# A graph-attention and expert kernel: the sums' wait for zeroed PSUM banks, on every second tile and one zeroing later

## The chip, the cores and the metric

The kernel runs on one core of a Trainium2 chip. The metric is the device time of one launch in microseconds (us), the median of several runs. TensorE (PE in the profile, PEld for its weight loads) multiplies matrices, VectorE (DVE), ScalarE (ACT) and GpSimd (POOL) work elementwise or gather, SyncE (SP) issues transfers. Each engine works through its own list of instructions in order, and waits on semaphores for the others.

## The reference

A graph layer over 6250 nodes and 100,000 edges sorted by destination, then an expert layer with eight experts of which each node uses two. What matters here is the graph layer's last step, a sum of messages over the edges of each destination node:

```
h = jnp.einsum('ni,hid->nhd', x, W)
...
alpha = jnp.exp(e_stable)
alpha_sum = jax.ops.segment_sum(alpha, dst, num_segments=N)
alpha_norm = alpha / (alpha_sum[dst] + 1e-08)
msg = alpha_norm[:, :, None] * h_src
out_h = jax.ops.segment_sum(msg, dst, num_segments=N)
...
for e in range(E):
    h = jax.nn.gelu(tokens @ w1[e] + b1[e], approximate=False)
    y = h @ w2[e] + b2[e]
    out = out + combine[:, e:e + 1] * y
```

## The kernel before

A first part (to about 144 us) normalizes x, multiplies it with the weights into a table of 260 columns per node in HBM, and cuts the edges into tiles of 128 that belong to blocks of 125 nodes. The second part works in 52 rounds of 16 tiles, 832 tiles in all. The loops of all engines run over a round `it` and a step `k` (the tile of that round), and the order in which the code lists the work of a step is the order on that engine; nothing else sets it.

In a round, GpSimd gathers the table rows of the edges for a round three ahead (L753, `ring`). VectorE and TensorE work out the softmax arguments of the next round in a chain that goes back and forth: TensorE's D (L1121, sixteen small matmuls at step 0), VectorE's `eC` (L803 to L807), TensorE's transpose (L1129, step 3), VectorE's scans, TensorE's L1132 (step 5), L1138 and L1139 (step 7), L1142 (step 9), VectorE's `arg`, ScalarE's exponentials (L1416 to L1418, step 10), VectorE's messages (L863, steps 11 to 14). At step k TensorE adds tile k into a PSUM bank: L1164, a matmul of the tile's one-hot matrix `oh` with its messages, 128 x 260, in float32, which the chip runs in two passes. It is called sum k below. Three banks `agg_ps` are taken in turn, by the block that a tile belongs to; the bank's number is loaded from a table.

ScalarE's `evacuate` at step k waits until sum k - 1 is done (semaphore `agg`), copies the bank of the tile before to `acc` (L1396), and zeroes the bank into which a coming block will be added (L1398, "zeroing k" below), which counts up `zr`. Each step has one copy and one zeroing, whether or not a block ends there. In front of sum 0 TensorE also waits for VectorE's rescaling of a bank (`rs`, L856), in front of sum 12 for a one-hot matrix. `zr` counts all zeroings of the kernel, so `zr` at least t means that the zeroing of step t - 1, over all rounds, is done.

From round 4 on the expert layer runs in the same steps, three rounds for each group of three blocks, 17 groups. TensorE's `hidden` (L1191, six matmuls) and `output` (L1237, four matmuls) stand between the sums, and ScalarE's GELU (L1427) between the zeroings; `prepare` (L1243, L1273, L1294, L1296) readies the next group's blocks. VectorE adds the outputs up (L998). Rounds 7, 8 and 9 are the first three with the experts' matmuls of a group in them, and the pattern repeats every three rounds until round 51. Rounds 28, 29 and 30 are such a set: it runs from 922.55 to 1003.16 us.

Of the kernel before, what the change touches and what calls it, by code (L numbers as in the profile page):

```python
# [22 lines left out]
def gnn_ffn_kernel(nc, x, src, dst, W, attn, W_out, rw, w1, b1, w2, b2, out):  # L23
# [46 lines left out]
    with ExitStack() as ctx:  # L70
# [26 lines left out]
        with ExitStack() as st:  # L97
# [3 lines left out]
            def sem(name):  # L101
                return st.enter_context(nc.semaphore("p_" + name))
# [469 lines left out]
        with ExitStack() as st:  # L572
# [3 lines left out]
            def sem(name):  # L576
# [71 lines left out]
            S = {n: sem(n) for n in (  # L648
                "lk init am zr otc D e eT x1m X CC CBp rho rT arg wm sc al oh msg rs agg ev "
                "w1c w1l on tt oc pj x1 va sq xk tu uh ul rt lgc dif exr cm ct cc cs b2 yb yd yi h1 gl y2 ya st tops").split()}  # L650
# [34 lines left out]
            with nc.Block() as block:  # L685
# [414 lines left out]
                def _(pe):  # L1100
# [50 lines left out]
                    def aggregate(b, k):  # L1151
                        t, q = b * BT + k, k // 4
                        if k == 0:
                            if b > 0:
                                pe.wait_ge(S["rs"], b)
                            else:
                                pe.wait_ge(S["oh"], QUADS - 1)
                        elif k == 12:
                            pe.wait_ge(S["oh"], QUADS * b + QUADS + (1 if b + 1 < NBAT else 0))
                        if t == 0:  # L1160
                            pe.wait_ge(S["am"], 1)
                        elif t > 1:
                            pe.wait_ge(S["zr"], t - 1)
                        T.matmul(bank_of[k // 8][k % 8], oh[:, (4 * b + q) % OHQ, k % 4, :], rings[b % RING][:, k, :],  # L1164
                                 start=False, stop=True, skip_group_check=True).then_inc(S["agg"], 1)

# [12 lines left out]
                    def edges(it, k):  # L1179
                        if it + 1 < NBAT:  # L1180
                            chain(it + 1, k)
                        if 0 <= it < NBAT:
                            aggregate(it, k)
# [346 lines left out]
```

## Time and profile before

| | us |
|---|---|
| runs (three), median | 1638.88 |
| runs, lowest and highest | 1637.24, 1646.97 |
| profiled execution | 1644.37 |
| its span, first to last instruction | 1642.6 |
| TensorE busy with matmuls | 1358.9 (83%) |
| VectorE busy | 1106.4 (67%) |
| ScalarE busy | 990.5 (60%) |
| GpSimd busy | 837.5 (51%) |

The span is 1.8 us shorter than the profiled execution's own time, which in turn is 5.5 us over the median of the runs. Matmuls are pipelined and their ends in the profile are modelled, so that rows of TensorE that follow each other overlap a little.

### The profile page before, as it was taken

To read this page: it belongs to the slowest core of one execution; us is meant where nothing else is said; L and a number is where in the kernel's file an instruction comes from. 1 tells how busy PE (TensorE), PEld (TensorE's weight loads), DVE (VectorE), ACT (ScalarE), POOL (GpSimd) and SP (SyncE) were. 2 spreads that over 40 slices of the span, in tenths; PEclk is the share of its full clock that TensorE was granted. 3 is DMA by queue.
4 is the path that set the end of the run, shared out by engine and by line. 5 is a ranking of instruction groups with operands and counts; after the bars stand their busy time and mean duration, and the time that the engine had idled before them with its cause. 6 is when DMAs were issued, how large, how long until landed. Compare 5 with 4: busy or idle time off the path is not lost.

```text
span 1642.6 us, 25322 instructions
## 1 busy us (share of the span) xinstructions
PE 1358.9 (83%) x7177; PEld 1114.8 (68%) x7177; DVE 1106.4 (67%) x3062; ACT 990.5 (60%) x2522; POOL 837.5 (51%) x886
## 2 busy tenths in 40 slices
PE   5741575578989888998999889899988888998998
PEld 3630343467777777777777777777777777777887
DVE  6522464667777777777676768687867677777643
ACT  3530444457666666766676767676767576767733
POOL 1237465656565555655555555555555555552000
PEclk9775566889999999999999999999999999999999
DMA  9355354333434343434343434343433333456000
GB/s 218 95 153 143 102 154 117 102 107 96 126 97 122 97 124 104 117 104 115 104 115 103 115 106 115 104 113 106 114 106 111 104 107 106 115 101 80 1 17 16
DMA packets 89793, 174.56 MB, mean 106 GB/s; under 512 B 22471, under 2 KB 56081, under 8 KB 89625
## 3 DMA queue, kind: packets, MB, share of 16 engines
q0 software_dynamic: 40448, 111.89, 26.8%
q1 hardware_dynamic: 48103, 60.78, 12.5%
q8 instruction: 60, 0.98, 0.2%
q14 instruction: 76, 0.62, 0.1%
q10 hardware_dynamic: 1106, 0.27, 0.1%
HBM read 159.26 MB, written 14.43 MB: 106 GB/s over the span
## 4 chain that ended last, share of the span: by engine, by line
PE 45%; ACT 14%; DVE 14%; another core or an unknown queue 11%; issue 8%; ACTq 2%; DVEq 0%
PE agg_ps L1164 14%; PE ob L1237 13%; PE hb L1191 10%; ACT acc L1396 4%; ACT agg_ps L1398 3%; PE ob L1273 2%; ACT hT L1427 2%; DVE ring L863 2%; DVE oh L798 2%; DVE y L998 1%; ACT L1427 1%; ACT L1409 1%; PE ob L1302 1%; ACTq L662 1%
## 5 line engine op out<-in xcount | busy, mean ns | idle before, releaser
L753 POOL DMA_INDIRECT ring<-table,srcE x832 | 805.4, 968 | 596.0 <-PE agg_ps L1164 294.7
L1164 PE MATMUL agg_ps<-ring,oh 128*128 128x260 f32 x1664 | 539.6, 423 | 32.4 <-ACT agg_ps L1398 15.0
L1396 ACT COPY acc<-agg_ps x831 | 307.6, 370 | 322.1 <-issue 123.1
L1237 PE MATMUL ob<-w_sb,hT 128*125 128x256 f32 x1600 | 413.6, 384 | 32.7 <-DVE y L998 16.2
L1164 PEld LDWEIGHTS agg_ps<-ring,oh 128*128 128x128 f32 x1664 | 305.6, 205 | 87.4 <-issue 27.3
L1237 PEld LDWEIGHTS ob<-w_sb,hT 128*125 128x125 f32 x1600 | 294.4, 188 | 96.5 <-issue 26.6
L1398 ACT COPY agg_ps<-zc 128x260 f32 x832 | 314.6, 378 | 28.6 <-issue 2.3
L863 DVE TENSOR_TENSOR ring<-ring,kbank 128x1024 f32<-128x1024 f32 x208 | 244.7, 1214 | 46.3 <-ACT ring L1417 44.8
L998 DVE SCALAR_TENSOR_TENSOR y<-ob,cmb,y 125x256 f32<-125x256 f32 x400 | 189.1, 476 | 100.0 <-remote 47.0
L1427 ACT ACTIVATE hT<-hb,b_sb 128x375 f32<-128x375 f32 (+1 forms) x272 | 154.0, 566 | 120.1 <-PE hb L1191 95.6
L1191 PE MATMUL hb<-xTh,w1l 128*128 128x376 f32 (+1 forms) x544 | 188.9, 429 | 0.0
L798 DVE TENSOR_TENSOR oh<-kbank,relE 128x512 f32<-128x512 f32 x208 | 141.0, 678 | 4.4 <-PE agg_ps L1164 2.4
L1191 PE MATMUL hb<-xTl,w1h 128*128 128x376 f32 (+1 forms) x544 | 138.5, 336 | 0.0
L1191 PE MATMUL hb<-xTh,w1h 128*128 128x376 f32 (+1 forms) x544 | 137.5, 335 | 0.0
L1191 PEld LDWEIGHTS hb<-xTh,w1l 128*128 128x128 f32 x544 | 103.7, 194 | 15.6
L803 DVE TENSOR_REDUCE dsum<-kbank 128x64 f32<-128x192 f32 x52 | 18.6, 358 | 139.4 <-remote 133.5
L1191 PEld LDWEIGHTS hb<-xTh,w1h 128*128 128x128 f32 x544 | 99.3, 192 | 0.0
L1191 PEld LDWEIGHTS hb<-xTl,w1h 128*128 128x128 f32 x544 | 99.0, 192 | 0.0
L1129 PE MATMUL kbank<-ident,eC 128*64 128x128 f32 x52 | 16.0, 308 | 89.9 <-DVE eC L807 63.4
L761 POOL TENSOR_TENSOR rstd<-mv,root_ 125x3 f32<-125x3 f32 (+1 forms) x17 | 14.8, 871 | 124.3 <-DVE mv L927 123.5
L1129 PEld LDWEIGHTS kbank<-ident,eC 128*64 128x64 f32 x52 | 5.9, 113 | 103.2 <-DVE eC L807 73.5
L486 PE MATMUL bank<-wcat,xnT 128*125 128x264 f32 x200 | 60.2, 429 | 14.5 <-issue 6.4
(285 smaller groups left out, 1461.8 us busy)
## 6 DMA issues: line engine op xcount, KB each, us to landing
OT<-relb_d SPq DMA_DIRECT2D x52, 512.0 KB
ring<-table,srcE POOLq DMA_INDIRECT x832
y<-in_x_dram SPq DMA_DIRECT2D x50, 125.0 KB
out_dram<-y SPq DMA_DIRECT2D x50, 125.0 KB
table<-hrow SPq DMA_DIRECT2D x25, 227.5 KB
acc<-in_x_dram SPq DMA_DIRECT2D x2, 1568.0 KB
acc<-in_L_ffn_w_dram SPq DMA_DIRECT2D x1, 2048.0 KB
w_sb<-in_L_ffn_w_dram SPq DMA_DIRECT2D x1, 2048.0 KB
```

The source lines that it names most:

```text
L486: m = T.matmul(bank[2 + b % 3][0:Q, 0:WIDE], xnT[:, b % 2, k, :], wcat[:, k, :], start=k == 0, stop=k == KC - 1)
L753: pool.indirect_dma_start(out=rings[b % RING][:, k, :], out_offset=None, in_=table[:, :], in_offset=bass.IndirectOffsetOnAxis(ap=srcE[:, t ...
L798: v.tensor_tensor(oh[:, (4 * b + q) % OHQ], iota_ps.unsqueeze(1).to_broadcast([P, 4, P]), relE[:, t0:t0 + 4].unsqueeze(2).to_broadcast([P, ...
L863: v.tensor_tensor(m, m, al.to_broadcast([P, 4, H, DH]), ALU.mult).then_inc(S["msg"], 1)
L998: v.scalar_tensor_tensor(y[0:Q, u, i, :], o[0:Q, 0:D], cmb[0:Q, u, i, e:e + 1], y[0:Q, u, i, :], ALU.mult, ALU.add).then_inc(S["ya"], 1)
L1164: T.matmul(bank_of[k // 8][k % 8], oh[:, (4 * b + q) % OHQ, k % 4, :], rings[b % RING][:, k, :], start=False, stop=True, skip_group_check= ...
L1191: t = T.matmul(out_, a, b_, start=j == 0, stop=j == len(terms) - 1)
L1237: t = T.matmul(o[0:Q, 0:D], hT[:, e % 2, f, cols], w2_sb[:, e, f, :], start=f == 0, stop=f == KC - 1)
L1273: t = T.matmul(ob1[0:Q, j * D:(j + 1) * D], oT[:, j, k, :], wout_sb[:, k, :], start=k == 0, stop=k == KC - 1)
L1396: A.copy(row_of[h][k % 8], closed[h][k % 8]).then_inc(S["ev"], 1)
L1398: A.copy(coming[h][k % 8], zc[:, 0:1].to_broadcast([P, ROW])).then_inc(S["zr"], 1)
L1427: A.activation(hT[:, e % 2, f, 0:w], hbank[f][:, 0:w], ACT.Gelu, bias=b1_sb[:, e, f:f + 1]).then_inc(S["gl"], 1)
```

## The change

One condition in `aggregate` is changed. Let t be the number of a tile over all rounds. Before, every sum from t = 2 on waits for `zr` at least t - 1. Now the sums of even t wait for `zr` at least t, and those of odd t have no wait on `zr`. A round has 16 tiles, so even t is even k.

```diff
                         if t == 0:
                             pe.wait_ge(S["am"], 1)
-                        elif t > 1:
-                            pe.wait_ge(S["zr"], t - 1)
+                        elif t > 1 and t % 2 == 0:
+                            pe.wait_ge(S["zr"], t)
                         T.matmul(bank_of[k // 8][k % 8], oh[:, (4 * b + q) % OHQ, k % 4, :], rings[b % RING][:, k, :],
                                  start=False, stop=True, skip_group_check=True).then_inc(S["agg"], 1)
```

415 sums (t = 2, 4, ... 830) wait for one more zeroing than before, 415 (t = 3, 5, ... 831) lose their wait. A waiting sum holds its weight load, which is issued first. No instruction of any engine is added, removed or moved. On TensorE, at the start of a round of the kind of round 29 (its D, then sums 0 to 3 with what stands between them), before the change:

```order
L1121 MATMUL kbank<-d3,OT 128x12 x15
L1164 MATMUL agg_ps<-ring2,oh 128x260 [waits e_zr,e_rs]
L1164 MATMUL agg_ps<-ring2,oh 128x260 [waits e_zr]
L1243 MATMUL ob1<-ident,xn 128x125 [waits e_ya]
L1243 MATMUL ob1<-ident,xn 128x125
L1164 MATMUL agg_ps<-ring2,oh 128x260 [waits e_zr]
L1191 MATMUL hb0<-xTh,w1l 128x376 [waits e_gl]
...
L1129 MATMUL kbank<-ident,eC 64x128 [waits e_e]
L1164 MATMUL agg_ps<-ring2,oh 128x260 [waits e_zr]
L1237 MATMUL ob0<-w2_sb,hT 125x256 [waits e_ya,e_gl]
```

The same place now:

```order
L1121 MATMUL kbank<-d3,OT 128x12 x15
L1164 MATMUL agg_ps<-ring2,oh 128x260 [waits e_zr,e_rs]
L1164 MATMUL agg_ps<-ring2,oh 128x260
L1243 MATMUL ob1<-ident,xn 128x125 [waits e_ya]
L1243 MATMUL ob1<-ident,xn 128x125
L1164 MATMUL agg_ps<-ring2,oh 128x260 [waits e_zr]
L1191 MATMUL hb0<-xTh,w1l 128x376 [waits e_gl]
...
L1129 MATMUL kbank<-ident,eC 64x128 [waits e_e]
L1164 MATMUL agg_ps<-ring2,oh 128x260
L1237 MATMUL ob0<-w2_sb,hT 125x256 [waits e_ya,e_gl]
```

Nothing moved: sums 1 and 3 lost their wait. Sum 2's wait, the third L1164, reads the same but asks for zeroing 1 now, where it asked for zeroing 0.

## Rows read from the trace of the kernel before

**Rows 1.** Page, costliest groups: count | busy us, mean ns | idle us before them, releaser.

```profile
L1164 PE MATMUL agg_ps<-ring,oh 128*128 128x260 f32 x1664 | 539.6, 423 | 32.4 <-ACT agg_ps L1398 15.0
L1396 ACT COPY acc<-agg_ps x831 | 307.6, 370 | 322.1 <-issue 123.1
...
L1398 ACT COPY agg_ps<-zc 128x260 f32 x832 | 314.6, 378 | 28.6 <-issue 2.3
...
L1427 ACT ACTIVATE hT<-hb,b_sb 128x375 f32<-128x375 f32 (+1 forms) x272 | 154.0, 566 | 120.1 <-PE hb L1191 95.6
```

**Rows 2.** Windows, middle and early rounds: us, busy by engine, PEclk, DMA share, GB/s.

```profile
352.00:1540.00 1188.00, 1068.38 (x5847) 893.58 (x5848) 880.02 (x2416) 804.91 (x2008) 667.35 (x690) 0.99 0.40 107
144.00:352.00 208.00, 119.76 (x462) 80.45 (x462) 107.36 (x271) 90.86 (x259) 122.96 (x128) 0.66 0.41 114
```

**Rows 3.** Windows, rounds 28 to 30, the same columns.

```profile
922.55:1003.16 80.61, 72.26 (x402) 60.58 (x403) 60.37 (x167) 54.79 (x138) 47.17 (x50) 1.00 0.39 111
```

**Rows 4.** Timeline, round 28, tile 4: start us, us, what [idle before <-releaser].

```profile
928.64 0.60 PE L1164 MATMUL agg_ps<-ring,oh 128*128 128x260 f32 x2
...
929.10 0.38 ACT L1398 COPY agg_ps<-zc 128x260 f32 x1
...
931.53 0.71 PE L1164 MATMUL agg_ps<-ring,oh 128*128 128x260 f32 x2 [0.33 <-issue]
```

**Rows 5.** Timeline, round 28, tile 12.

```profile
940.61 0.30 PEld L1164 LDWEIGHTS agg_ps<-ring,oh 128*128 128x128 f32 x2 [0.28 <-issue]
...
941.22 0.38 ACT L1398 COPY agg_ps<-zc 128x260 f32 x1
```

**Rows 6.** Timeline, round 29, tile 2.

```profile
950.55 0.60 PE L1164 MATMUL agg_ps<-ring,oh 128*128 128x260 f32 x2
...
951.68 0.50 PE L1191 MATMUL hb<-xTh,w1h 128*128 128x376 f32 x2
...
951.96 0.38 ACT L1396 COPY acc<-agg_ps  x1 [2.37 <-PE agg_ps L1164]
...
952.37 0.38 ACT L1398 COPY agg_ps<-zc 128x260 f32 x1
...
952.89 0.30 PE L1129 MATMUL kbank<-ident,eC 128*64 128x128 f32 x1 [0.71 <-issue]
```

**Rows 7.** Timeline, round 29, tile 14.

```profile
969.92 0.61 PE L1164 MATMUL agg_ps<-ring,oh 128*128 128x260 f32 x2
...
970.28 0.38 ACT L1398 COPY agg_ps<-zc 128x260 f32 x1
...
972.99 0.45 PE L1237 MATMUL ob<-w_sb,hT 128*125 128x256 f32 x1 [1.00 <-issue]
```

**Rows 8.** Timeline, round 30, tile 2.

```profile
978.71 0.60 PE L1164 MATMUL agg_ps<-ring,oh 128*128 128x260 f32 x2
...
979.15 1.03 PE L1237 MATMUL ob<-w_sb,hT 128*125 128x256 f32 x4
...
980.38 0.38 ACT L1398 COPY agg_ps<-zc 128x260 f32 x1
...
980.90 0.30 PE L1129 MATMUL kbank<-ident,eC 128*64 128x128 f32 x1 [0.73 <-DVE eC L807]
```

**Rows 9.** Timeline, round 30, tile 14.

```profile
997.37 0.60 PE L1164 MATMUL agg_ps<-ring,oh 128*128 128x260 f32 x2
...
998.36 0.38 ACT L1398 COPY agg_ps<-zc 128x260 f32 x1
...
998.79 0.71 PE L1164 MATMUL agg_ps<-ring,oh 128*128 128x260 f32 x2
...
1002.05 0.41 PE L1121 MATMUL kbank<-d,OT 128*128 x10 [1.52 <-DVE oh L798]
```

**Rows 10.** Timeline, round 3 of the first seven, tile 2.

```profile
252.01 0.38 ACT L1398 COPY agg_ps<-zc 128x260 f32 x1
...
252.53 0.42 PE L1129 MATMUL kbank<-ident,eC 128*64 128x128 f32 x1 [6.50 <-DVE eC L807]
```

## The prediction

> **What bounds the kernel now.** I read the page's groups first, then the busy time by stage, then the timeline of three rounds in which the pattern repeats. In what follows sum k is TensorE's L1164 for tile k of a round, and zeroing k is ScalarE's L1398 in its step k of the same round. Before, sum k waits for zeroing k-2. In the changed kernel an even sum waits for zeroing k-1, and an odd sum waits for none. The page's row of the sums says that TensorE stood idle 32.4 us in all in front of them, of which 15.0 us ended with a zeroing [rows 1]: the present wait is nearly free. From 352 to 1540 us TensorE is busy 1068.38 of 1188.00 us, and its clock is at 0.99; ScalarE is busy 804.91 us [rows 2]. So the long middle is TensorE's, with 120 us of idle time in it, or 8.35 us in the three rounds from 922.55 to 1003.16 us [rows 3]. ScalarE is no bound by its share, but it runs behind TensorE, and today it may be a tile further behind than after the change. What the change costs is therefore the lateness of zeroing k-1 against sum k, for even k, less what TensorE idles shortly afterwards anyway.
>
> **The wait that is removed.** Odd sums lose a wait. Its price can't be over the 15.0 us of [rows 1] for odd and even together, since the next even sum asks for more than the odd one did. Below nothing is excluded, because nothing is added there. I take zero: where an odd sum waits today, the even one in front of it waits for the same zeroing after the change.
>
> **The wait that is moved forward**, place by place in rounds 28 to 30, which stand for 15 such groups of three (rounds 7 to 51). TensorE works in order, so behind a waiting sum its own hidden, output and step matmuls queue, and VectorE's chain and ScalarE's GELUs wait for those.
>
> Round 28, tile 4: zeroing 3 ends at 929.10 + 0.38 = 929.48, the sum started at 928.64 [rows 4]. With its weight load behind the wait it starts about 929.6, 0.95 late. TensorE's idle time before tile 6, 0.33 us, gives that much back: 0.6 stays.
>
> Tile 10 of round 28, and tile 6 of rounds 29 and 30, have a loop: hidden matmuls, GELU, copy, zeroing, next even sum. The ScalarE part is 566 + 370 + 378 ns = 1.31 us and some handovers [rows 1]; TensorE has a sum and an output between, 998.79 - 997.37 = 1.42 us from one sum to the next [rows 9]. Between nothing and 0.5 us each; I take 0.25, since the two are nearly equal.
>
> Round 28, tile 12: weight load 940.61, zeroing 11 ends 941.60 [rows 5], 1.0 late as it stands. But this zeroing is behind ScalarE's exponentials and a GELU that waited for TensorE's hidden matmuls, so ScalarE will come some 0.7 later by itself (the 0.6 and 0.25 above). TensorE is then 1.7 behind, which contains the earlier shifts and is the round's sum.
>
> Round 29, tile 2, the dearest: ScalarE waited 2.37 us for TensorE's sums before its copy at 951.96, and zeroing 1 ends at 952.75; sum 2 ran at 950.55 [rows 6]. It moves to about 952.83, 2.3 late. In front of L1129 TensorE has 0.71 us idle now. Sum 2 and the hidden matmuls take 952.18 - 950.55 = 1.63 us, so L1129 moves from 952.89 to about 954.45: 1.55 is left. L1129 feeds VectorE's softmax chain, so the chain moves with it. With the loop, 1.8.
>
> Round 29, tile 14: zeroing 13 ends at 970.66, the sum was at 969.92, 0.85 late with its load; 1.00 us of idle time follows before the output at 972.99 [rows 7] and takes it. Between 0 and 0.85, I take 0.
>
> Round 30, tile 2: the same as in round 29 with output matmuls in place of hidden ones. Zeroing 1 ends 980.76, sum 2 moves from 978.71 to 980.84, and with 1.47 us of work (979.15 + 1.03 - 978.71) L1129 comes at 982.2 instead of 980.90 [rows 8], 1.3 late. Tile 14: zeroing 13 ends 998.74 against 997.37, 1.4 late, and 1.52 us of idle time before L1121 at 1002.05 covers it, unless what that waits for moves along [rows 9]. Between 0 and 1.4, I take 0.4, nearer to the cover. With the loop 1.95.
>
> The group: 1.7 + 1.8 + 1.95 = 5.45 us, times 15 = 82 us. **The first seven rounds** are paced otherwise, with TensorE idle 6.50 us before L1129. Zeroing 1 ends at 252.39, L1129 starts at 252.53 [rows 10]. Sum 2 now stands between, 0.8 us at the slow clock, so L1129 is 0.7 later: 7 x 0.7 = 5 us. **Sum:** 1644.37 + 82 + 5 = 1731 us for the profiled execution. That execution is 5.5 us above the median of the runs, 1638.88, so in runs as shown 1726 us, 5.3% slower.
>
> **A page weighed against the rows.** The largest terms hang on when TensorE's sums are known to be done. By the modelled ends, sums 0 and 1 are over when sum 2 starts at 950.55, while ScalarE's copy, which needs only sum 0, got its signal 1.4 us later [rows 6]. The Trainium skill, Perfetto Trace Analysis, section Tensor Engine Instruction, states that the end reported for TensorE is estimated from the instruction's size and that the semaphore is pushed only after PSUM acknowledges. The trace agrees, and adds that it can be over a microsecond here. If the modelled ends were the truth, zeroing 1 would end near 951.4 and both tile 2 terms would vanish into the idle time, leaving 2.6 us a group, 39 us and a time of 1683. I go by the signal.
>
> **Rivals.** (a) *Given back.* The idle time at the end of rounds 29 and 30 (1.00 and 1.52 us, [rows 7, 9]) and before L1129 belongs to signals that do not move with TensorE. Then the shifts of the rounds are swallowed there too: 5.45 - 2.5 - 1.0 for the chain, about 2 us a group, 30 + 5 us, 1674. For it: VectorE and ScalarE have spare time. Against: what they wait for is mostly TensorE's own result. (b) *Nothing given back.* All six places at their full lateness, 1.0 + 1.0 + 2.3 + 0.85 + 2.1 + 1.4, and 1 us for the loops, 9.65 us a group: 145 + 5, 1789. For it: VectorE's chain shifts too, and ScalarE's lag is renewed by each GELU. Against: 8.35 us of idle time a group is there to be used. (c) *The clock.* In the rounds from 144 to 352 us TensorE is busy 119.76 of 208 us and its granted clock averages 0.66, a mix of the levels of 1.2 and 2.4 GHz, against 0.99 in the middle [rows 2]. The added waits lower its share in the middle from 0.90 to about 0.84. If that costs a twentieth of the clock, 1068 us of work grow by about 50, on top of the forecast: 1776. The Trainium skill, TensorE: Matmul & The Clock Gate, section What's actually happening, says that the array runs at 1.2 GHz after idling and at 2.4 GHz once busy; by it the longer stalls in rounds 29 and 30 would be the ones to fall. (d) *No effect.* Once TensorE has waited for a few zeroings it is no longer ahead, the later even waits find theirs done, and what was lost lies inside idle time: 1640. Against it stand three zeroings that end over 1 us after their sum began. (e) *Faster.* The odd sums' loads start at once, and the 15.0 us of waiting for zeroings goes without a new one: 1624. It decides from the point at which every even sum finds zeroing k-1 done; [rows 4 to 9] show six that do not, so it has little for it.
>
> **How the numbers follow.** Forecast 0.54 (1726, own range 1700 to 1760), given back 0.17, nothing given back 0.12, clock 0.08, no effect 0.06, faster 0.03. The range 1666 to 1790 holds the forecast, most of (a) and (b), and (c); what is left out is (d), (e) and the tails. A difference of 1%, 16 us, is about what a measurement of this kernel tells from none. Slower by more than that: the first four less the low tail of (a), 0.88; same 0.09; faster 0.03.
>
> **What would show it.** In the changed kernel's profile the idle time in front of L1164 that ended with a zeroing should go from 15.0 us to 150 us or more, and lie at tiles 2, 4, 12 and 14. TensorE's busy time should stay within 1%. L1129 should come right after hidden or output matmuls in rounds of the kinds of 29 and 30, with its idle time gone. A group of three rounds should take 86 us instead of 80.6. If it takes 83 or less, (a) is right; if the granted clock of the middle is under 0.97, (c) is in it. The forecast is wrong in kind if the signals of sums 0 and 1 come earlier once TensorE has less queued behind them, since that lateness was measured with it running ahead.

## The result and the profile after

The changed kernel takes 1722.07 us (median of 4 runs, 1713.95 to 1725.43) beside 1638.06 us for the kernel before (4 runs, 1633.63 to 1646.97): a ratio of 1.0487, with a 95% interval of 1.0458 to 1.0516. The forecast was 1726. The profiled execution took 1720.34 us, 76.0 more than that of the kernel before.

The page of the changed kernel, costliest groups, as in [rows 1]: count | busy us, mean ns | idle us before them, releaser.

```profile
L753 POOL DMA_INDIRECT ring<-table,srcE x832 | 805.5, 968 | 671.7 <-PE agg_ps L1164 409.6
L1164 PE MATMUL agg_ps<-ring,oh 128*128 128x260 f32 x1664 | 555.3, 430 | 200.9 <-ACT agg_ps L1398 152.6
L1396 ACT COPY acc<-agg_ps x831 | 307.1, 370 | 334.1 <-PE agg_ps L1164 118.3
```

The idle time in front of the sums went from 32.4 to 200.9 us, and what of it ended with a zeroing from 15.0 to 152.6. The copies and zeroings themselves are as long as before.

The changed kernel's waits of TensorE: waited for, us in total, times, longest us.

```profile
PE agg_ps L1164 <- ACT agg_ps L1398: 152.6, 89, 22.1
PE agg_ps L1164 <- issue: 47.8, 57, 2.1
PE kbank L1121 <- issue: 26.0, 7, 12.7
PE kbank L1129 <- issue: 17.9, 1, 17.9
```

The same view of the kernel before, for the two step matmuls that idled most:

```profile
PE kbank L1129 <- DVE eC L807: 63.4, 17, 19.3
PE kbank L1129 <- issue: 26.4, 11, 19.2
PE kbank L1121 <- DVE oh L798: 18.6, 14, 1.8
PE kbank L1121 <- issue: 17.7, 6, 11.9
```

So not all of the new waiting is new. L1129's idle time fell from 89.8 to 17.9 us: TensorE now waits before it gets there, in front of sum 2. One such wait alone is 22.1 us long and lies in the first seven rounds, which have become hardly longer: from the start of round 0 to the start of round 7 it was 203.2 us before and is 204.5 now (149.89 to 353.12, and 150.34 to 354.85). The 76 us came behind that. The last sum ends at 1643.19 us in place of 1567.20.

Windows of the changed kernel: the middle, the early rounds, rounds 28 to 30; columns as in [rows 2, 3].

```profile
352.00:1620.00 1268.00, 1103.95 (x5890) 909.16 (x5889) 887.51 (x2428) 811.16 (x2014) 668.24 (x691) 0.97 0.37 100
144.00:352.00 208.00, 112.41 (x439) 71.00 (x440) 107.60 (x271) 91.83 (x260) 122.99 (x128) 0.71 0.41 114
...
967.26:1053.81 86.55, 75.02 (x409) 61.71 (x405) 60.19 (x164) 54.11 (x135) 48.91 (x50) 0.98 0.37 104
```

The group of three rounds takes 86.55 us in place of 80.61. TensorE is busy 75.02 in it where it was 72.26, and idle 11.5 where it was 8.35. Over the whole program it is busy 1383.5 us where it was 1358.9, 1.8% more.

The same from the start of round 7 to the start of round 49, which is fourteen groups of three and the same work in both kernels; first before, then after:

```profile
353.12:1495.95 1142.83, 1026.33 (x5628) 859.03 (x5629) 846.75 (x2324) 772.09 (x1925) 665.04 (x688) 0.99 0.41 109
354.87:1566.82 1211.95, 1054.85 (x5634) 868.69 (x5632) 847.99 (x2320) 773.63 (x1923) 663.55 (x686) 0.97 0.38 103
```

These fourteen groups take 69.1 us more. TensorE's idle time makes 40.6 us of that (116.5 before, 157.1 after), and 28.5 us is longer busy time at a lower granted clock. So a group is 4.9 us longer, of which 2.9 are idle time and 2.0 busy time.

Timeline of the changed kernel, round 29, tile 2, beside [rows 6]: start us, us, what [idle before <-releaser].

```profile
998.73 0.36 DVE L803 TENSOR_REDUCE dsum<-kbank 128x64 f32<-128x192 f32 x1 [0.88 <-PE kbank L1121]
1000.18 0.38 ACT L1396 COPY acc<-agg_ps  x1 [2.39 <-PE agg_ps L1164]
1000.59 0.38 ACT L1398 COPY agg_ps<-zc 128x260 f32 x1
1001.02 0.30 PEld L1164 LDWEIGHTS agg_ps<-ring,oh 128*128 128x128 f32 x2 [2.35 <-ACT agg_ps L1398]
...
1002.26 0.51 PE L1191 MATMUL hb<-xTh,w1h 128*128 128x376 f32 x2
...
1002.61 0.27 PE L1129 MATMUL kbank<-ident,eC 128*64 128x128 f32 x1
```

It is the picture of [rows 6] with the sum on the other side of the wait. ScalarE's copy still comes 2.39 us after it was free, zeroing 1 ends at 1000.97, and 0.05 us later the load of sum 2 starts, 2.35 us late. L1129 now follows the hidden matmuls without idle time.

Round 29, tile 14, beside [rows 7]:

```profile
1019.91 0.38 ACT L1398 COPY agg_ps<-zc 128x260 f32 x1
1020.34 0.30 PEld L1164 LDWEIGHTS agg_ps<-ring,oh 128*128 128x128 f32 x2 [1.36 <-ACT agg_ps L1398]
...
1023.45 1.10 PE L1237 MATMUL ob<-w_sb,hT 128*125 128x256 f32 x4 [0.94 <-DVE y L998]
```

The sum's weight load waits 1.36 us for zeroing 13, and the idle time before the output matmuls, which was to take that up, is still there in this round: 0.94 us, beside 1.00 in [rows 7].

One idle time is not the whole cover, though. From the start of sum 14 to the next round's sum 0, TensorE idled 2.08 us in round 29 before and idles 1.47 now. In the mean of the rounds of this kind (rounds 7 to 50) it was 1.73 and is 0.75; in the kind of round 30 it was 1.49 and is 0.18. So most of the wait at tile 14 is taken up behind it.

To price all places and not three, I worked out from the trace of each kernel how long TensorE idles in front of sum k and how long the rounds are from sum 0 to sum 0. Means over rounds 19 to 51, in us; only places over 0.15 are named:

```
                  kind of round 28                  kind of round 29      kind of round 30
before            k0 .43, k6 .41, k12 .23           k3 .20                -
after             k0 .34, k2 .94, k4 .37, k6 .38,   k2 1.69, k14 1.28     k2 1.31, k8 .20,
                  k12 1.09, k14 .50                                       k14 1.03
round (7 to 51)   27.02 -> 29.21 (+2.2)             27.57 -> 29.18 (+1.6) 26.79 -> 27.97 (+1.2)
```

A group of three is 5.0 us longer. Every even sum that waited over 0.15 us started within 0.15 us of the end of its zeroing (0.05 in the median), and no odd sum waited in these rounds.

### The profile page after: what moved, and what is told of

Read it like the earlier page. It is cut to its first block, busy times and chain, and to the rows that moved or that the text cites. A ratio compares the mean times of both kernels' runs of the same rounds, so it can differ in the third digit from the quotient of the medians.

```text
span 1718.5 us, 25322 instructions
## 1 busy us (share of the span) xinstructions
PE 1383.5 (81%) x7177; PEld 1117.8 (65%) x7177; DVE 1108.3 (64%) x3062; ACT 993.6 (58%) x2522; POOL 837.5 (49%) x886
## 4 chain that ended last, share of the span: by engine, by line
PE 48%; ACT 19%; another core or an unknown queue 9%; issue 9%; DVE 6%; ACTq 3%; DVEq 0%
PE agg_ps L1164 17%; PE ob L1237 12%; PE hb L1191 11%; ACT acc L1396 6%; ACT agg_ps L1398 5%; ACT hT L1427 3%; PE ob L1273 2%; ACT L1409 2%; ACT L1427 2%; ACTq L662 1%; DVE ring L863 1%; ACTq L667 1%; DVE oh L798 1%; DVE y L998 1%
## 5 line engine op out<-in xcount | busy, mean ns | idle before, releaser
L1164 PE MATMUL agg_ps<-ring,oh 128*128 128x260 f32 x1664 | 555.3, 430 | 200.9 <-ACT agg_ps L1398 152.6
L1164 PEld LDWEIGHTS agg_ps<-ring,oh 128*128 128x128 f32 x1664 | 291.5, 203 | 302.5 <-ACT agg_ps L1398 168.6
L1237 PE MATMUL ob<-w_sb,hT 128*125 128x256 f32 x1600 | 418.9, 388 | 11.3 <-DVE y L998 8.7
L1237 PEld LDWEIGHTS ob<-w_sb,hT 128*125 128x125 f32 x1600 | 302.7, 192 | 67.6 <-issue 16.2
L803 DVE TENSOR_REDUCE dsum<-kbank 128x64 f32<-128x192 f32 x52 | 18.6, 357 | 115.2 <-remote 105.1
L812 DVE TENSOR_TENSOR_SCAN FRP<-flags,kbank 64x128 f32<-64x128 f32 x52 | 21.4, 411 | 90.8 <-PE kbank L1129 87.4
L486 PE MATMUL bank<-wcat,xnT 128*125 128x264 f32 x200 | 60.4, 430 | 14.5 <-issue 10.1
L1427 ACT ACT_TABLE_LOAD x50 | 64.2, 1283 | 9.6 <-PE hb L1191 8.6
```

The source lines that it names most:

```text
L486: m = T.matmul(bank[2 + b % 3][0:Q, 0:WIDE], xnT[:, b % 2, k, :], wcat[:, k, :], start=k == 0, stop=k == KC - 1)
L1237: t = T.matmul(o[0:Q, 0:D], hT[:, e % 2, f, cols], w2_sb[:, e, f, :], start=f == 0, stop=f == KC - 1)
L1427: A.activation(hT[:, e % 2, f, 0:w], hbank[f][:, 0:w], ACT.Gelu, bias=b1_sb[:, e, f:f + 1]).then_inc(S["gl"], 1)
```

## The experiments

They ran on three chips, with the kernel before timed on each: 1461.66 us (7 runs, 1461.08 to 1463.89), 1626.23 (13 runs, 1615.89 to 1631.20) and 1628.36 (7 runs, 1616.90 to 1631.01). The first chip needs 10% less time for the same program. That was the largest surprise of the study, and it turned out to be a second experiment. Ratios are only taken within one chip. The expectations of the first four kernels were written for a kernel before of 1638 us, so it is their differences, and not their times, that can be compared with what was measured.

### First chip: which sums the wait stands before

**Tile 2 alone** has the new wait, all others keep theirs.

```
                         elif t > 1:
-                            pe.wait_ge(S["zr"], t - 1)
+                            pe.wait_ge(S["zr"], t if k == 2 else t - 1)
```

> The wait for the zeroing of its own number stands in front of sum 2 of each round alone; every other sum, even and odd, waits as in the kernel before. By the prediction's terms, tile 2 is worth 1.55 us in the second kind of round, 1.3 us in the third and nearly nothing in the first, 15 times each, and 0.7 us in each of the seven early rounds: 43 + 5 us, so about 1686 us. Against it: if one moved wait a round is enough to take TensorE's lead over ScalarE away, and the others only find it gone, this kernel is as slow as the changed one, about 1722 us. If tile 2's cost is given back by the idle time that follows, it stays within 1640 to 1650 us.

Measured: 1474.15 us, ratio 1.0083 (1.0066 to 1.0100), +12.5 us. The idle time in front of sum 2 is 0.10, 0.21 and 0.01 us in the three kinds of round. The place that I had called the dearest costs little here: 12.5 us where 48 was expected.

**Tiles 12 and 14 alone.**

```
+                            pe.wait_ge(S["zr"], t if k in (12, 14) else t - 1)
```

> The wait for the zeroing of its own number stands in front of sums 12 and 14 of each round alone; all others wait as before. By the prediction's terms tile 12 costs 1.0 less 0.28 us of idle time in the first kind of round, and tile 14 is covered in the second kind and costs 0.4 us in the third: about 1.1 us a group, 17 us in all, 1655 us. The rival reads the changed kernel's profile: TensorE idles there 1.1 + 0.5 + 1.3 + 1.0 us a group in front of sums 12 and 14, and if all of that is cost the time is 1638 + 58 = 1696 us.

Measured: 1514.85 us, ratio 1.0355 (1.0329 to 1.0380), +53.2 us. TensorE idles 1.34 us before sum 12 and 0.50 before sum 14 in the first kind of round, 1.28 before sum 14 in the second and 0.56 in the third. The cost is near the 58 us of the rival, not the 17 of the prediction's terms.

**All even sums, with the odd waits kept** as they were.

```
+                            pe.wait_ge(S["zr"], t if k % 2 == 0 else t - 1)
```

> Even sums wait as in the changed kernel, and odd sums keep the wait of the kernel before. The prediction took the removed waits at zero, since the even sum in front has waited for the same zeroing: the time of the changed kernel, 1722 us. The rival is that a wait costs by itself, satisfied or not, so that 415 of them more are worth some ns each; 20 ns each would make 8 us, 1730 us.

Measured: 1537.70 us, ratio 1.0521 (1.0504 to 1.0539), +76.0 us. TensorE idles 0.00 us in front of every odd sum in all three kinds of round. Nor does an odd sum start later for its wait: from the start of the instruction in front of it to its own it is 109 ns behind L1129, 170 behind a hidden matmul, 216 behind an output matmul and 219 behind a sum (medians of rounds 19 to 51), the same in this trace and in that of the changed kernel, whose odd sums have no wait. So a wait that is already met costs nothing that can be seen, and taking it away brings nothing. Of the 76.0, tile 2 and tiles 12 and 14 make 65.7; 10.3 is left for the other even tiles, if the places simply add.

**The other parity:** odd sums wait for the zeroing of the step in front, even ones for none.

```
+                        elif t > 1 and t % 2 == 1:
+                            pe.wait_ge(S["zr"], t)
```

> The same change with the other parity: odd sums wait for the zeroing of their own number, and even sums have no wait on zeroings. If the cost is the lateness of each zeroing against its sum less the idle time behind it, parity matters: in rounds 28 to 30 of the kernel before the odd places late by over 0.5 us are tiles 1, 3, 5, 11 and 13 of the first, 3 and 15 of the second, 1, 3 and 15 of the third, with 4.3 and 3.8 us at the two tiles 15 (about 2 us each after the idle time there). That makes some 7 to 8 us a group and 1745 to 1760 us. The rival is that half the allowance costs the same wherever it is taken: 1722 us.

Measured: 1546.34 us, ratio 1.0577 (1.0553 to 1.0601), +84.7 us. The idle time has moved to tiles 5 (1.30), 11 (.86), 13 and 15 (.26, .30) of the first kind and to tile 15 of the second and third (1.17, .60). So it matters little which of two neighbours waits: 84.7 us beside the 76.0 of the even tiles, a tenth more and clear of the noise, but far from the 107 us and more that the expectation's lateness would make. What costs is that a wait with one step of slack stands where there were two.

### Why tile 2 is cheap on this chip

The difference between the chips shows at the sixteen small matmuls of L1121, whose result VectorE reduces in L803. VectorE may start when it sees the semaphore update that stands behind the last of them. Timeline of the kernel before, round 29:

```profile
948.97 0.55 PE L1121 MATMUL kbank<-d,OT 128*128 x16
...
951.92 0.36 DVE L803 TENSOR_REDUCE dsum<-kbank 128x64 f32<-128x192 f32 x1 [2.21 <-remote]
```

Timeline of the kernel with the wait at tile 2 alone, on the first chip, the same round:

```profile
832.12 0.55 PE L1121 MATMUL kbank<-d,OT 128*128 x16
...
832.75 0.34 DVE L803 TENSOR_REDUCE dsum<-kbank 128x64 f32<-128x192 f32 x1
833.24 0.38 ACT L1396 COPY acc<-agg_ps  x1 [0.50 <-PE agg_ps L1164]
...
833.65 0.38 ACT L1398 COPY agg_ps<-zc 128x260 f32 x1
834.08 0.30 PEld L1164 LDWEIGHTS agg_ps<-ring,oh 128*128 128x128 f32 x2 [0.45 <-ACT agg_ps L1398]
```

From the modelled end of the matmuls to VectorE it is 951.92 - 949.52 = 2.40 us on the one and 832.75 - 832.67 = 0.08 on the other. The semaphore's own update comes 2414 ns (median of 52 rounds) after the modelled end in the trace of before, 5 to 8 us in most of the first seven rounds and once 21, and 14 ns in the trace of the first chip. (The traces of the slower chips lack some records of updates: before has 666 for the 832 sums, the first chip's has all 832. Those of L1121 are complete in both, and VectorE's starts agree with them.) TensorE goes on working through it, but the updates of the sums queued behind are late too and then come together: in an early round of before the burst ends at 269.19, its update comes at 277.29, and those of three instructions behind it at 277.34, 277.38 and 277.42. That is why ScalarE copies tile 0 so late there. VectorE's waits in front of L803, one line each from the two kernels' answers for that line, first before:

```profile
remote: 133.5, 36
```

then the first chip:

```profile
PE kbank L1121: 4.7, 9
```

The profile can name no releaser for the long ones, as no instruction ends at that time. With the signals on time TensorE is nearly without idle time in the middle. Window of the kernel with the wait at tile 2 on the first chip:

```profile
300.00:1370.00 1070.00, 1035.41 (x5821) 881.22 (x5820) 870.29 (x2394) 794.39 (x1991) 658.26 (x683) 1.00 0.44 117
```

That is 34.6 us in 1070, or 2.4 in a group, where [rows 3] have 8.35. My reading is that late signals make zeroing 1 late and so tile 2 dear, and leave idle time at the end of rounds in which a wait at tile 14 can hide: behind tile 14 it is 1.7 and 1.5 us in before, in the second and third kind of round, and 0.1 and 0.2 here. On time, tile 2 is cheap and tiles 12 and 14 pay in full. No kernel with the wait at tile 2 was run with and without late signals on one chip, so this rests on the comparison of chips, and on one trace that is told of at the end of the experiments.

### Second chip: repeats, and ScalarE's table loads

**Before and after, unchanged, once more:**

> The kernel before, unchanged, for its trace beside the others of this call: in the last call it took 1461.66 us where the first result had 1638 us, and its trace there is not to hand. If the 177 us are TensorE's signals that come late after D and after the transposes of the second kind of round (1.4 to 2.9 us each, and 5 to 8 us in the first seven rounds), then a trace at 1460 us has none of them, and one at 1640 us has them all. If the chips differ by a clock or by the transfers, the signals are as late in both and the busy times differ.

> The changed kernel, unchanged, on the chip of this call. Beside a kernel before of 1460 us: 1535 us, ratio 1.052, as with the odd waits kept. Beside one of 1638 us: 1722 us, ratio 1.049. By the prediction's terms alone, without the late signals the two tile 2 terms (43 us) should be missing, 1505 us; if it is 1535, tiles 12 and 14 cost about 30 us more than they were given.

Measured: before 1629.50 us in its profiled execution; after 1693.97 (1685.62 to 1696.87), ratio 1.0430 (1.0385 to 1.0475), +67.7 us. The signals of L1121 are late again (median 1896 ns in before). The change costs somewhat less here than in the result; the two intervals just overlap. The same fourteen groups as in the result, before and after:

```profile
347.81:1481.68 1133.87, 1030.90 (x5635) 865.72 (x5631) 844.32 (x2323) 770.99 (x1925) 662.65 (x688) 0.98 0.40 110
346.34:1532.84 1186.50, 1040.26 (x5634) 856.83 (x5631) 848.04 (x2320) 773.04 (x1923) 664.25 (x687) 0.99 0.38 105
```

TensorE's idle time grew by 43.3 us here (103.0 to 146.2) and by 40.6 in the result, nearly the same. What differs is the busy time: 9.4 us more here, with the clock a little higher after the change, and 28.5 more there, with the clock lower.

**No table loads between ScalarE's functions.** Zeroings 11 and 13 stand behind ScalarE's exponentials, and a load of 1283 ns comes at every change between GELU and exponential. In both kernels the five exponentials are replaced by copies, so that the softmax weights are not exponentials any more; everything else stands.

```
-                        A.activation(ex[0:Q, 0:n, :], dif[0:Q, 0:n, :], ACT.Exp)
+                        A.activation(ex[0:Q, 0:n, :], dif[0:Q, 0:n, :], ACT.Copy)
...
```

> The kernel before with a copy in place of each exponential of the second part on ScalarE (the attention weights, their rescaling factor and the router's, so these numbers are not exponentials), which takes away the table loads of 1.28 us, two a round. The allowance of two zeroings should hide them: within 1% of the kernel before if ScalarE's lag costs it nothing, up to 3% less if the loads are on VectorE's chain already (the one in front of the exponentials is early, the one before the GELU of step 12 is not waited for by that chain).

> The same edit in the changed kernel. If the late zeroings 11 and 13 are late because of the table loads that stand in front of them on ScalarE (steps 9 and 12), the moved waits at tiles 12 and 14 find them done, and the changed kernel with copies is only 1 to 2% over the kernel before with copies, in place of 5%. If the loop of hidden matmuls, GELU, copy and zeroing makes them late, the 5% stays.

Measured: 1614.32 us for before without loads, ratio to before 0.9942 (0.9912 to 0.9971), and 1674.79 for after without them, 1.0292 (1.0240 to 1.0344). Between the two it is 1.0375 where with loads it is 1.0430. The idle time before sums 12 and 14 is gone (0.00 to 0.03 us), but before sum 2 it is 1.79 and 1.45 in the second and third kind, and before sums 4 and 6 of the first .62 and .61. So the loads make zeroings 11 and 13 late, and without them most of the cost stands elsewhere: 60.5 us of 67.7 are left, a difference that the noise of these runs could hide, and not the 1 to 2% that were expected if the loads were the cause.

### Third chip: the places once more, with late signals

**Tile 2; tiles 12 and 14; the even tiles that are left,** each alone, with the edits above and

```
+                            pe.wait_ge(S["zr"], t if k in (0, 4, 6, 8, 10) else t - 1)
```

> Sum 2 alone waits for the zeroing of its own number, as in the first of the experiments, which ran where no signal of TensorE came late (1461.66 us before) and cost 12 us. Where the kernel before takes about 1630 us, D's signal comes 1.4 to 2.9 us late in two rounds of three, and by the prediction's terms the same edit costs 43 + 5 us: about 1675 us beside 1630. If tile 2's cost is not the late signal, it is 12 us here too. Beside a kernel before of 1462 us it repeats 1474 us.

> Sums 12 and 14 alone. Without late signals they cost 53 us. Beside a kernel before of 1630 us the idle time behind tile 14, where the signals after the transposes come late, covers part: 17 us by the prediction's terms, 53 us if nothing is covered. The sum of this, of tile 2 alone and of the other places is the changed kernel's 68 to 84 us if the places only add, and more if one place's stall takes another's away.

> Sums 0, 4, 6, 8 and 10 alone wait for the zeroing of their own number. By the prediction's terms: 0.6 us at tiles 4 and 6 of the first kind of round and 0.25 us for each of three loops, 1.35 us a group, 20 us in all. The rival takes the lateness in the kernel before with nothing given back (1.0, 0.7 and 0.3 us in the first kind, 0.7, 0.2 and 0.4 in the second, 0.2 in the third): 3.5 us a group, 52 us.

Measured: tile 2 1657.71 us, ratio 1.0215 (1.0156 to 1.0273), +29.4. Tiles 12 and 14 1651.07, 1.0149 (1.0095 to 1.0203), +22.7. The rest 1642.86, 1.0102 (1.0060 to 1.0144), +14.5. Together 66.6 us, beside 67.7 for the whole change on the second chip, whose kernel before takes 2 us less; each of the three has an interval of 7 to 10 us to either side, so that the agreement is closer than it could be told. With late signals tile 2 costs about twice what it costs without them, or more (29.4 and 12.5), and tiles 12 and 14 about half or less (22.7 and 53.2). The page's row for the sums of the kernel with the wait at tile 2:

```profile
L1164 PE MATMUL agg_ps<-ring,oh 128*128 128x260 f32 x1664 | 546.8, 427 | 122.1 <-ACT agg_ps L1398 98.4
```

and on the first chip:

```profile
L1164 PE MATMUL agg_ps<-ring,oh 128*128 128x260 f32 x1664 | 529.3, 415 | 23.3 <-ACT agg_ps L1398 21.7
```

**The burst itself.** In the kernel before, the sixteen matmuls of 12 columns of L1121 become two of 96 columns. They take the first block's operand for all tiles, so D holds other numbers; nothing else differs.

```
-                        for j in range(8):
-                            t = 8 * half + j
-                            m = T.matmul(D_ps[:, t * 3 * H:(t + 1) * 3 * H], OT[:, t * P:(t + 1) * P], block_of[half][j],
-                                         start=True, stop=True)
+                        m = T.matmul(D_ps[:, 8 * half * 3 * H:8 * (half + 1) * 3 * H], OT[:, 8 * half * P:(8 * half + 1) * P],
+                                     d3[:, 0:8 * 3 * H], start=True, stop=True)
```

> The kernel before with D as two matmuls of 96 columns in place of sixteen of 12 (so D holds wrong numbers), a signal at its end as before. If the burst of sixteen small matmuls is what the late signals follow, D's signal comes with its end in every round, and beside a kernel before of 1630 us this one takes 1500 to 1560 us. If the lateness has another cause, such as the gathers in flight, the signals stay late and the time is within 1% of the kernel before. Beside a kernel before of 1462 us it tells nothing, within 1%.

Measured: 1574.44 us (1568.51 to 1587.27), ratio 0.9693 (0.9637 to 0.9748), 54 us less, and so a smaller gain than the 1500 to 1560 us expected. Its timeline in a round of the same sort:

```profile
922.91 0.25 PE L1119 MATMUL kbank<-d,OT 128*128 128x96 bf16 x2
923.53 0.35 DVE L803 TENSOR_REDUCE dsum<-kbank 128x64 f32<-128x192 f32 x1
```

and VectorE's waits in front of L803:

```profile
issue: 5.4, 14
remote: 4.9, 2
```

The update after D now comes 14 ns after the modelled end (median; 9 of the 52 have no record), on a chip where it took 1.7 us with the wait at tile 2. D's own busy time is 0.30 us a round less, 15.6 us in 52 rounds, so the larger part of the 54 us should be the signal's; what the fourteen matmuls fewer bring besides was not measured by itself. It doesn't bring this chip to the first one's 1461.66: updates after other matmuls are still late in this trace.

This trace also bears on tile 2. In rounds of the kind of round 29, zeroing 1 ends 0.33 us (median) after sum 2 has started. On the same chip with D as it was it is 1.44 and 2.14 us, in the kernels with the waits at tiles 12 and 14 and at the other even tiles, and it is 2.24 in before. On the first chip, with the waits at tiles 12 and 14, it is 0.33. So in this kind of round the late zeroing 1 goes away with D's late signal. In the kind of round 30 it is not as clear: 0.72 us with D in two matmuls, and 1.99, 0.56, 2.04 and -0.21 in the others, in the same order.

## Why the prediction was right, and where its terms were off

**Right: what binds.** An even sum starts when zeroing k-1 ends, at tiles 2, 4, 12 and 14 as listed, and TensorE's queue moves with it. The group grew by 5.0 us where 5.45 was worked out (5.94 in rounds 28 to 30 alone). The idle time ended by zeroings is 152.6 us where 150 or more was said, with the reservation above that some of it is L1129's old wait under another name. L1129's idle time is gone in the middle; 17.9 us of it remains, in one early wait.

**Right: the odd waits are worth nothing.** With them kept, no odd sum waits at all, and the cost on the first chip, 1.0521, is no smaller than the whole change's elsewhere, 1.0487 and 1.0430. As no kernel on the first chip has them removed and the even ones in place, that last comparison bounds them only across chips. What settles it is the odd sums' distance from the instruction in front of them, which is the same with the wait and without.

**Off, and hidden by the total: what the 5 us of a group are made of.** The 5.45 us were to be stalls, with TensorE's busy time within 1%. It grew by 1.8%. Of the 4.9 us that a group grew from round 7 to 49, 2.9 were idle time and 2.0 busy time, so the stalls were put too high, by some 2 us a group, and the busy time, which stood at nothing, filled the gap. Two parts of the busy time can be estimated from the trace. The granted clock stood at its lower level for 31 us of these rounds before and for 65 after; 34 us at half the clock lose 17 us of work at most, 1.2 a group. And the two matmuls of a sum take 0.71 us behind a wait where they take 0.60 without one (1020.34 above, [rows 4]), and 68 more sums waited, which is 7 us or 0.5 a group. On the second chip the clock did not fall, and the whole change cost 67.7 us. That the total came within 4 us of the forecast is luck to that extent.

**Off: single terms.** From the third chip, in us of the whole program: tile 2 was put at 48 (1.55 and 1.3 a group, and the early 5) and measures 29.4. Tiles 12 and 14 were put at 19 (what tile 12 adds to the 0.6 and 0.25 before it in the 1.7, 0.85, and 0.4) and measure 22.7. Tile 4 and the loops were put at 20 (0.6 and three times 0.25) and measure 14.5. Only the first of these differences is clear of the noise, the other two are not. These steps lie behind the terms.

- Tile 2 of the first kind of round was held free. It has 0.94 us of idle time now. In [rows 4 to 9] I looked for late zeroings in three rounds only; in the kernel before, zeroing 1 ends over 0.1 us after the start of sum 2 in 4 of the 15 rounds of this kind, of which round 28 is none. With the wait at tile 2 alone, on the third chip, the idle time there is 0.29 us, so most of the 0.94 seems to come from the other moved waits. By which path is not shown.
- Tile 14 of rounds 29 and 30 was taken at 0 and 0.4, covered by the idle time behind it [rows 7, 9]. That was about right. In rounds 7 to 50 the wait before the sum is 1.24 and 1.20 us, and the idle time from there to the next sum 0 shrank by 0.98 and 1.31, so that 0.3 us and nothing are left. What the three rounds hid is how much of it there was: in round 29 more stood behind the tile than the 1.00 us that I used (2.08 in all).
- More was given back than the places that I priced: 2.97 us of idle time before even sums in the second kind of round make it only 1.6 longer, and 2.54 in the third only 1.2. Besides L1129 and the end of the round, TensorE's idle time fell from 0.79 to 0.32 us before the output matmuls of step 8 in the second kind, and from 0.48 to 0.22 before L1138 in the third (rounds 7 to 50).
- The first seven rounds were put at 5 us and cost 1.3. The wait of sum 2 took the place of L1129's there instead of coming on top: both end after the same late signals.
- A slip in the sum: with sum 2 at 980.84 and 1.47 us of work, L1129 comes at 982.31 and not at 982.2, so that the term of round 30, tile 2, is 1.4 us and not 1.3, and the forecast 1.5 us too low.

The prediction stayed within 4 us of the result because these cancelled, and because the busy time grew; the terms were not that good.

**TensorE's reported ends.** The largest terms hung on whether sums 0 and 1 were done at their modelled ends, which would have given 1683, or when ScalarE got the signal. The signal was right, and the first chip shows the other case: with updates 14 ns after the modelled end tile 2 costs 12.5 us in place of 29.4. The Trainium skill, Perfetto Trace Analysis, section Tensor Engine Instruction, states that the end is estimated and the semaphore is pushed once PSUM has acknowledged. The traces agree that the update comes after the reported end, by 2.4 us on one chip and 0.014 on another for the same instruction. Whether it is PSUM's acknowledgement that is late, no run here shows.

**The rivals.** *The clock*: the middle stands at 0.97 in the changed kernel and at 0.99 in [rows 2]. Over the whole profiled execution the means are 0.928 and 0.930, and TensorE's busy time grew 24.6 us where that rival wanted 50 on top of 82. So it is there with about half its size. But it isn't shown to be an effect of the change: on the second chip the clock of the same fourteen groups went from 0.98 to 0.99, with 43.3 us more of idle time. The Trainium skill, TensorE: Matmul & The Clock Gate, section What's actually happening, has the array at 1.2 GHz after idling. The two traces of the result agree with it, with more idle time and a lower clock, and the two of the second chip do not. *Given back* (group 83 or less) and *nothing given back* (9.65 more) are both refuted for the group at +5.0, though each is partly there: the idle time before even sums grew by 8.1 us a group (9.1 against 1.1 in the table), while all of TensorE's idle time grew by 2.9, so that about 5 us were given back, more than the prediction allowed. *No effect* and *faster* are out on every chip.

**Open.** What makes TensorE's updates late on some chips was not found. With late signals their release often falls 0.7 to 0.9 us after the last packet of one of GpSimd's gathers (117 of the 370 late updates of sums in before, where about a tenth would fall there by chance), but no kernel was made that moves the gathers, so this is an observation and not a cause. The slower chips' traces also hold only half as many records of semaphore updates (12,073 in before, 25,218 on the first chip with the wait at tile 2); whether this and the lateness have one cause was not tested. Nor was the kernel before traced on the first chip; its row there is that of the kernel with the wait at tile 2, 0.8% longer.

No version beat both kernels and computed the same thing. The two that were faster than before show where time may be had: D in fewer, wider matmuls (54 us), and ScalarE without table loads (12 us).

## What to carry to other kernels

Before a wait is moved, count the producer's steps of slack at each place and in every kind of round, and price the place as its lateness less the idle time behind it, both as means over all rounds of a kind and with all of the idle time up to the next such place: one row of round 29 showed the idle time behind tile 14 untouched (1.00 and 0.94 us), where the mean of fifteen rounds and all rows had given most of the wait back. A wait that is already met cost nothing here, so giving one up pays for nothing. Compare idle time and busy time by themselves, since a total can be right with both of them wrong. And time the kernel before on the very chip of the comparison: the same wait at tile 2 cost 12.5 us on one chip and 29.4 on another, those at tiles 12 and 14 53.2 and 22.7, while the whole stayed between 4.3 and 5.2%.

## What the runs showed of the hardware

- The same program took 1461.66 us on one chip and 1626 to 1638 us on the others. In the traces (before, and the first chip's kernel with the wait at tile 2, 173 us shorter) 42 us of the difference are TensorE's busy time (1358.9 and 1316.5 us, at a mean clock of 0.930 and 0.955) and the rest is idle time. The instructions are the same; what differs is when TensorE's semaphore updates come after its matmuls' modelled ends.
- On the slower chips, the update after sixteen bf16 matmuls of 12 columns came 2.4 us behind their modelled end in the median of before, and up to 21 us; after two of 96 columns it was 14 ns. On the first chip it was 14 ns after the sixteen too. TensorE itself ran on meanwhile.
- A semaphore wait that was already met added nothing to the distance between a sum and the matmul in front of it (109 to 219 ns with it and without).
- A ScalarE table load took 1283 ns, 101 times in each kernel with exponentials; taking 99 of them away brought 0.6% of the time (0.3 to 0.9), 12 us for 127 us of loads.
